# Maximum and sum of the later softmaxes by ScalarE, head by head, in the last three pairs of a chain of four transformer blocks

## The reference

```
x = x + Wo0 * attention(groupnorm(x), context)              # 8 heads of 64 (channels as tokens: 256x256 scores)
x = x + tanh(gate) * Wo1 * attention(x, layernorm(context))  # 16 heads of 16
h = rmsnorm(attention(x; keys of context and of x) + x);  x = MLP(h) + x
x = x + attention(layernorm(x))                              # self, masked
x = x + attention(layernorm(x), context)                     # cross, masked
x = x + MLP(layernorm(x))
```

## Time and profile before

| | us |
|---|---|
| median of 3 runs | 1304.58 (1303.95 to 1304.62) |
| profiled execution | 1303.31 |
| its span, first to last instruction | 1301.4 |
| mean granted clock of TensorE | 0.987 of full speed |
| TensorE busy | 1238.8 (95%) |
| VectorE busy | 1026.2 (79%) |
| ScalarE busy | 869.2 (67%) |
| GpSimd busy | 565.5 (43%) |

### The profile page before, as it was taken

The page is one execution under the profiler, slowest core; times in us unless marked ns, Lnnn a source line. Parts: engine busy times, 40 slices in busy tenths (PEclk is TensorE's granted clock), DMA queues, the critical chain, the costliest instruction groups (busy, mean ns, idle before and its releaser), DMA issues.

```text
span 1301.4 us, 35231 instructions
## 1 busy us (share of the span) xinstructions
PE 1238.8 (95%) x13116; PEld 963.6 (74%) x13116; DVE 1026.2 (79%) x2452; ACT 869.2 (67%) x2287; POOL 565.5 (43%) x977
## 2 busy tenths in 40 slices
PE   6999999999999999999999999999999999999775
PEld 4766778777777877777786777868777787868554
DVE  4778887888978787888878788787888888696753
ACT  3666677776767777776766776768676777766441
POOL 2553454264444526345344535443354453442321
PEclk9999999999999999999999999999999999999896
DMA  8100000000000000000000000000000000000000
GB/s 323 35 18 19 2 24 3 22 8 7 18 11 19 7 22 8 18 7 11 19 7 22 8 6 19 12 18 7 23 8 6 19 7 6 3 6 2 6 5 5
DMA packets 23589, 25.78 MB, mean 20 GB/s; under 512 B 10624, under 2 KB 22912, under 8 KB 23168
## 3 DMA queue, kind: packets, MB, share of 16 engines
q1 hardware_dynamic: 23424, 23.55, 5.8%
HBM read 21.44 MB, written 2.10 MB: 18 GB/s over the span
## 4 chain that ended last, share of the span: by engine, by line
PE 79%; DVE 9%; issue 5%; ACT 4%; POOL 2%; DMA 0%; SPq 0%; POOLq 0%; DVEq 0%; ACTq 0%
PE bank L687 10%; PE bank L953 8%; PE bank L513 8%; PE attended L642 8%; PE bank L627 7%; PE bank L962 7%; PE bank L693 5%; PE bank L721 5%; PE bank L502 4%; PE bank L747 4%; PE bank L710 3%; PE bank L734 3%; PE bank L680 2%; PE bank L421 2%; PE bank L738 2%
## 5 line engine op out<-in xcount | busy, mean ns | idle before, releaser
L614 POOL TENSOR_SCALAR p_a<-p_a,rec_a 128x256 f32<-128x256 f32 x512 | 244.3, 495 | 187.7 <-DVE rec_a L569 187.5
L600 ACT ACTIVATE p_a<-bank,nmax_a 128x256 f32<-128x256 f32 x512 | 236.8, 476 | 68.2 <-DVE nmax_a L563 67.5
L563 DVE TENSOR_REDUCE nmax_a<-bank 128x2 f32<-128x512 f32 x256 | 167.8, 678 | 12.6 <-PE bank L513 11.8
L627 PE MATMUL bank<-ident,p_a 128*128 128x128 f32 x1024 | 143.0, 277 | 5.6 <-POOL p_a L614 2.7
L627 PEld LDWEIGHTS bank<-ident,p_a 128*128 128x128 f32 x1024 | 114.2, 142 | 33.6 <-issue 25.2
L513 PE MATMUL bank<-k_a,q_a 64*128 64x256 f32 x1024 | 137.5, 395 | 1.2 <-ACT q_a L580 0.7
L642 PE MATMUL attended<-p_a,v_a 128*64 128x256 f32 x1024 | 133.7, 390 | 2.6 <-DVE v_a L474 1.1
L513 PEld LDWEIGHTS bank<-k_a,q_a 64*128 64x128 f32 x1024 | 92.4, 186 | 27.6 <-issue 18.8
L600 ACT ACTIVATION_READ_ACCUMULATOR p_a<-bank,nmax_a 128x1 f32 x512 | 106.0, 207 | 0.0
L642 PEld LDWEIGHTS attended<-p_a,v_a 128*64 128x64 f32 x1024 | 64.1, 136 | 55.2 <-issue 21.9
L675 ACT ACTIVATE p_a<-bank 128x512 f32<-128x512 f32 x128 | 75.8, 602 | 29.6 <-PE bank L627 28.9
(11 more groups left out here) (260 smaller groups left out, 2987.1 us busy)
## 6 DMA issues: line engine op xcount, KB each, us to landing
wb<-in_wb SPq DMA_DIRECT2D x1, 4096.0 KB, 12.3
wc<-in_wc SPq DMA_DIRECT2D x1, 4096.0 KB, 24.8
xc<-in_x SPq DMA_DIRECT2D x16, 128.0 KB, 2.7
xc<-in_ctx SPq DMA_DIRECT2D x16, 128.0 KB, 2.9
c_top<-in_ctx SPq DMA_DIRECT2D x16, 128.0 KB, 2.7
k_c<-in_ctx SPq DMA_DIRECT2D x16, 128.0 KB, 2.1
res_a<-in_x SPq DMA_DIRECT2D x16, 128.0 KB, 2.2
out<-y_out SPq DMA_DIRECT2D x16, 128.0 KB, 1.7
```

What stands on the lines that cost most here:

```text
L563: dve.tensor_reduce(nmax_a[:, n, e, :], ps[:, :].rearrange("p (q k) -> p q k", q=KT), AX.X, ALU.max, negate=True).then_inc(A.s["max"], 1)
L600: last = act.activation(p_a[:, j % 2, n, e, qt, :], ps[:, qt * D:(qt + 1) * D], ACT.Exp, bias=nmax_a[:, n, e, qt:qt + 1], accum_out=sum_a[ ...
L614: last = pool.tensor_scalar(p_a[:, j % 2, n, e, qt, :], p_a[:, j % 2, n, e, qt, :], rec_a[:, n, e, qt:qt + 1], 1.0, ALU.mult, ALU.mult)
L627: last = nc.tensor.transpose(ps[:, kt * D + qt * P:kt * D + (qt + 1) * P], p_a[:, j % 2, n, e, qt, kt * P:(kt + 1) * P], ident[:, :])
```

## The change

In the pairs from 13 on, in all four later attentions, VectorE writes the maxima negated and takes nothing off. ScalarE takes each group's exponentials in 8 instructions, one a head, each with the head's negated maximum as bias and the head's sum as accumulated output, straight into T.sum. VectorE's sum falls away; it only takes the reciprocal, waiting for the exponentials. TensorE's transposes wait for the exponentials instead of the sum. ScalarE has one further wait, for the reciprocals of the pair before. ORDER and BANK are new strings, made for this; up to pair 12 they differ from the old ones by small swaps, in the last three pairs by more.

```diff
+BY_HEAD = {"b": 13, "e": 13, "c": 13, "f": 13}
 ...
             for r in range(KT):
                 for c in range(blocks):
                     yield
-                    pe.wait_ge(T.s["sum"], T.at(i, "sum", r + 1))
+                    if by_head(T, i):
+                        pe.wait_ge(T.s["exp"], T.at(i, "exp", r + 1))
+                    else:
+                        pe.wait_ge(T.s["sum"], T.at(i, "sum", r + 1))
 ...
+        def by_head(T, i):
+            return i >= BY_HEAD[T.name]
 ...
-                dve.tensor_reduce(T.max[:, r, :], v.rearrange("p c h k -> p h c k"), AX.XY, ALU.max).then_inc(T.s["max"], 1)
+                dve.tensor_reduce(T.max[:, r, :], v.rearrange("p c h k -> p h c k"), AX.XY, ALU.max,
+                                  negate=by_head(T, i)).then_inc(T.s["max"], 1)
+                if by_head(T, i):
+                    continue
 ...
-                dve.tensor_reduce(T.sum[:, r, :], heads_of(T, r).rearrange("p c h k -> p h c k"), AX.XY, ALU.add).then_inc(T.s["sum"], 1)
-                yield
-                dve.wait_ge(T.s["sum"], T.at(i, "sum", r + 1))
+                if not by_head(T, i):
+                    dve.tensor_reduce(T.sum[:, r, :], heads_of(T, r).rearrange("p c h k -> p h c k"), AX.XY, ALU.add).then_inc(T.s["sum"], 1)
+                    yield
+                    dve.wait_ge(T.s["sum"], T.at(i, "sum", r + 1))
 ...
-                act.wait_ge(T.s["sub"], T.at(i, "sub", r + 1))
-                act.activation(T.p[:, r, :], T.p[:, r, :], ACT.Exp).then_inc(T.s["exp"], 1)
+                if by_head(T, i):
+                    act.wait_ge(T.s["max"], T.at(i, "max", r + 1))
+                    if i:
+                        act.wait_ge(T.s["rec"], T.at(i, "rec", 0))
+                    v = heads_of(T, r)
+                    for h in range(HB):
+                        last = act.activation(v[:, :, h, :], v[:, :, h, :], ACT.Exp, bias=T.max[:, r, h:h + 1], accum_out=T.sum[:, r, h:h + 1])
+                    last.then_inc(T.s["exp"], 1)
+                else:
+                    act.wait_ge(T.s["sub"], T.at(i, "sub", r + 1))
+                    act.activation(T.p[:, r, :], T.p[:, r, :], ACT.Exp).then_inc(T.s["exp"], 1)
```

More of the change, by code:

```diff
@@ L103 @@
[L103 to L112, removed]
@@ new lines @@
+        "nksnnnakaaaaaddaadddddaadkkdkdnkddsnddkkaaddksksddaaddadkdaadddnnaabddbdnadbdddaandddbbdbadkkbaedddeeeedeadddd"
+        "daddanneaebeebaaenakekdddndadbdgaggbbdggbdabcddeccceeceededdddaaaddccdaddceedaceeadefddfefnandbddbdaafdafndfdk"
+        "kkdnfagkkkkkgbgaddgghbddbcabcccbhcehdeeheecddcdecaaddadcdddhaddfannefeeeaabdebaaendddnddgdadgfddgggadffdfdaadd"
+        "fdckacckkcdckkkadbkkdddcddchaabcbdbcaabhefbdeeeedbehfnnddhheeeeaeadefddddndaddaaagdggddndffgfgkddfkckaaddddkkk"
+        "kbcddcckbhcbabanhbbchencdeeeedaecdhbcadhdeeeeaeadnfeafndddadgdfdggdaaggddffddafckkkcccfkkdbddddcdahkkbkbabhhbd"
@@ new lines @@
+        "ceaceeeehebddbdahcnnaeeceeaenddfeaddnfdgddafddggaaddggffaadfddckfkkcckkckbdacdkkddhdbdbabhhbcaeheeeedenanchddb"
+        "dacbeecdeendeadfeafnddfgddaaddggadfdfgdfdgkaakfkcddddkkkkkcbccddaahdbcdbaabhbhecceeeecenndcddhhdabeebeedaeaded"
+        "fdandfdganddfddaadggdadgfgfafdckfkkcckkkcbaahkkddddhhabbhdbcddbhbeddeeeeccdeabcnaacnddeedfdefaefddanddedaaffef"
+        "dddkfdkkndgdkkggbkggkaakddchdbabcccbdchbdeheeeeccaecabddbhhceedeaeaefnfeandfddgddggaadngfdgfddfaknkkfdddcdkkcc"
+        "cahbdhchkbkkhbhbdaccbcaaeceeeedddedaadddadffebedbeedaenneafdddagnagdddgffggnfddfckkkccckhkchhbkhkdhakdbddbcabc"
@@ new lines @@
+        "dcbdeceeeedddeddaafdfnaneeeebaebaendadnagddggfddagddgadfdafdfckkkccfckkkkkbdhcdhhdbddhbhbacbcaeceeeeceaadddddd"
+        "deefeeaefaefddnaanabddgbddaggffdgngddfankkkfcddakkcccbdkckkdhbabddhabccdhbcedheeeecheaafddfddddaefddeeeanebnfb"
+        "eddfdaaadgfaddgkakgfadkddhgdgkkdddcdabkckkhbccbhcbddahbdeheeeccedecddddcddeebfeefbfeefgfgfgkgfkkgkkkkbckhchhcc"
+        "bbcbhbhecceeeececeefeeefefgfggfggfkfccchchchhhccccfffffffhhhhh"),
+    "act": (
+        "knnakaaaasadaadaaaadaakdaakdkaadkkaaaaddaaaaadnnabadbaaadbadbabbaabdaakeadaeaddeaenneaebaeebaaaeaakaddaagbbgbb"
+        "gdaabcaeadcedcdeaacccaaaaeceeddaeeaefaanandbdfbfafafaafadkkkgaakkggbabdahbbcabachedhccecdccaaeaaddeaafnaeaeeea"
+        "nbadaebaaadgdaagdgffffaafdaadcakaakkckackcddcbchbbcbaabaaaefbaadehbhnedeneeeeaeaaddaafagafdaaggffafadkkckaaddk"
+        "kbbcbhbabacncabachehcdneacdbeeeeeeaaeaafaaaddagaggdffaadffaaafckkkckddbahbkbbcbacahechcaaebdbdaecneneeeeaeafaa"
+        "adgdaafggfaadaffadafaackkkkcabdkbdhbbcbaachcheaaenancedbdecbeeeeaaefaaadgdaafaafggffdafadkakakacdkkcdbabhbaaba"
+        "baaccecchhecnnddeebeebaeeaaeaadfadagaaddaafggfaaaffafckkkkchakabdbdahabbahbdbecdceccaabcneneaeefaeadeaadaafedf"
+        "ffaafdkaakkgdkggbbkaadhcbbaacbheccheccacbdaaebeeedeeaaefaanangdfggafadfafafakkkacddkchaabhbbhkbccbacccaeaaedde"
+        "adafaeebedaeeabaeannadgaaffdgfgfaafckkkchkhchckbbdabdabcbcaaceeddaafeneneeeebaeabaadagdaagagaadffdfafafcakkkac"
+        "kkhdbbhbdhbccbcacaecaaeaaeddeeefeeaeaaadnanabdgabffaggffaadfakkkcdakaacbbhkbbccdaahbccaceahdeaafeddeeaeeeafnfa"
+        "ebafbndfdaaagfaaagkakadgkadahkdcabbkbbachbhdcaecaecccddeefbeeeebeffgffgfgkkkkkchbbcbbhbhccecceceeeeeefefgffggf"
@@ new lines @@
+        "bbbdbabnbbabbdabaannnnabaakbbaaaddeaeeeeeeeeeeaeddeaeenadeeanenaaanaaaenannnaaeegkgkgdgdagnkknabbbbbnbbnbbgbba"
+        "gabangcccabdcabadbcaceecccceeeceeeeceeceeaadccaccdaaceeaaeacedeacafffdfaaaedafeegffffngafnffkffafnfafdndaaagng"
+        "nngnaafdnffhnaaknhnhaknhkkkkgbbbbbgbbababdbbgbcacccaacbcabbhccccchccececcceeceeddeeeeeaaecaaeacefdfdfefaaheeaa"
+        "deannfannaaaaeaaeengngngngddngaannnnaadgffffadfgfffkfgffafaccccafaadafaadfhhhchcaacccckcckacbbbcckcbbcbbcbbdbb"
+        "kdaabkckdaacbfafffbaabaaheeaeeeedeeeeeheefeeneedenhnaaneaaeeffffgggfdndnagafgknaanfaffaafafgfgaandadnnnnfagccc"
@@ new lines @@
+        "fffffffffhhhhhhh"),
+    "pool": (
+        "ssknaaaaaaaakaakaankkaaaaaaaaaaakanabbaaaeagaaeakeeaaaaaagnaabbccaaegacaeccaaccaaeeffaaaakffkffaagaanhkhaakcbc"
+        "baacaeagcceccaaffaaeeaaaagnaakffaakcffcaaaahhcaackckccbbaaffeagaeaaeeaakffkgaaaaffaanaccahhkkcbbccaageccaaefee"
+        "faaaangaakkffaaffcaacaachkhckcbbegccaaeaaeeffaagaankffkaaffaaccaaaahhckkccbbaacgceeaafeefaagaankffkaaaaffaacch"
+        "ahakkcbbccaaaaegccefeefaaaagaanakffakaaffaacchhckkaabbaaccegeccaaffeeaakffkaaffaaagahnahakkccbbcaaccegeccaaeef"
+        "faaaagkkffffacacaanhhakacaacckbbccegffaeaaaeeaaaakgkffaaffcacanhhckcckbbaccaaeagffeeeaagaanaakffkaacffcaachahk"
+        "akccbbccegaaeaaffeeaakkagffaaaffaaccnhhkaacaakccbbccaaegaaeffkffeekaaffaagaaaahhaackcaakbcbaaccegeccaaffeekffk"
+        "gffhhckckcbbccegcceffeekfgfffcchhcccccffffffhh"),
```

93 lines of the change are left out of this document (33 added, 60 removed).

## The result

The changed kernel takes **1320.89 us** (1319.9 to 1322.07), the kernel before 1304.26 us beside it on the same chip: a ratio of 1.0127, 95% interval 1.0112 to 1.0142. It is slower, as forecast, but by 16.6 us where the sum had 7.3, and so just outside the range given. The profiled execution took 1322.07 us, the slowest of its four, against 1303.31 before; so what is read from the two traces adds up to 18.7 us and not to 16.6.

What follows compares the result with a forecast made beforehand. TensorE was taken to bound the kernel, almost gapless in the middle, so the waits of the last pairs decide. Terms 0.8 + 2.1 + 0.9 + 1.1 + 3.4 - 1 = +7.3 us on the 1304.6 median gave 1312 us, range 1300 to 1320.

Steps and rivals of the forecast that it cites:

- two signs of being wrong: Stated refutations: a head takes under 0.24 us, or TensorE has no gap behind the output product of stage e, pair 14.
- E14/F13: Stage e of pair 14, f of 13: exponentials behind the last copy leave TensorE 4.1 us idle, not 0.7: +3.4 us.
- E15/C14: Stage e of pair 15 beside c of 14: 5.9 us less in the stretch, 7.0 us more ahead: +1.1 us.
- The price of a head: ScalarE's exponential for one head, start to start: 0.29 us, 2.4 a group of eight; in stage e 0.34, 2.85 a group.
- G of 15: Stage g of pair 15 beside f of 14: two table loads saved against longer exponentials and queueing: +0.9 us.
- C of 15: Stage c of pair 15, alone at the end: second group's transposes begin at 1262.4 instead of 1260.3: +2.1 us.
- F of 15: Stage f of pair 15, nothing beside it: second group's exponentials end later, delaying transposes and product: +0.8 us.
- H of 15: Last stage of pair 15, up to the span's end: no term of its own, counted as 0.
- Elsewhere: Pairs 12 to 14: work drawn forward and VectorE freed, -1 us; further up and at the start 0, within 2.
- Rival 1: Faster: short exponentials and fillers, heads of 0.23 to 0.24 us, about -3 us, 1301 us; chance 0.19.
- Rival 2: Order absorbs it: stall in stage f of pair 13 filled, start and middle give 2 back, 1304 to 1306 us; chance 0.14.
- Rival 3: Accumulator reads don't overlap with 64-column exponentials: 0.52 us a head, +18 us, 1330 us; chance 0.05.

Runs made afterwards that it cites:

- spares in both kernels: Never-read matmuls put ahead of tail steps: 73 in the changed kernel, 1307.46 us; 46 in the kernel with new order to stage e of pair 12, 1291.98 us.
- new tail: Changed kernel with old order and banks up to stage e of pair 12, new ones with exponentials by head only behind it: 1331.21 us, ratio 1.0195.
- new head: Kernel before with new order and banks up to stage e of pair 12, old ones behind, softmax unchanged: 1300.11 us against 1305.12, ratio 0.9964.

## Why the prediction was right and wrong

**Direction and places** were right: the waits moved from VectorE's sums to ScalarE's exponentials, and the gap behind e14's product is there. Neither of the two signs of being wrong came: a head is not under 0.24 us, and that gap exists. TensorE's gaps behind 1173 us grew by 9.0 us, where 7 were forecast. TensorE after, between e14's projection and g14:

```profile
1167.58 1.13 PE L751 MATMUL bank<-wb,e_yT 128*128 128x256 f32 x4 [0.93 <-DVE e_yT L801]
1171.31 1.12 PE L725 MATMUL bank<-ident,f_p 128*128 128x128 f32 x4 [2.60 <-ACT f_p L823]
...
1173.96 1.12 PE L725 MATMUL bank<-ident,f_p 128*128 128x128 f32 x4 [0.68 <-ACT f_p L823]
```

In brackets stands the idle time before: 2.60 and 0.68, and 0.16 ahead of g14's transposes between them (not shown), 3.4 us where 4.1 were forecast. The way to it was not quite the one laid out. ScalarE ended e14's copy at 1167.07 and then waited for f13's maximum, which waited for GpSimd's mask:

```profile
1166.48 2.48 POOL L857 TENSOR_TENSOR f_p<-f_p,m_add 128x512 f32<-128x512 f32 x2
1167.78 0.69 DVE L783 TENSOR_REDUCE f_max<-f_p 128x8 f32<-128x512 f32 x1 [0.25 <-POOL f_p L857]
1168.50 0.35 ACT L823 ACTIVATE f_p<-f_p,f_max 128x64 f32<-128x64 f32 x1 [1.43 <-DVE f_max L783]
```

**The step that failed is twofold: the two terms between e14 and e15 were too small, and no term had the clock.** E14/F13 and E15/C14 were laid out at +4.5 us together. They measured +13.9, and +9.9 at full clock with spares in both kernels. All terms behind e14 come to 8.3 us, where the new tail costs 15.5 at full clock. On top of that stand 5.3 us for TensorE's clock, for which the sum had nothing, since every term is counted in waits at the durations of the rows of before. The sum missed by no more than 9.3 us because the new head gives 5.0 back, where the sum had -1 for pairs 12 to 14 and nothing, within 2, for what stands ahead of them; that is luck.

What the clock does is seen behind each new gap. f13's transposes take 1.12 us for four, where eight took 1.44 in the earlier trace rows, and g14's first half 3.62. From e14's projection to e15's the stretches in the section on the result are 14.06 us apart, of which gaps are 6.5 (14.71 us of idle against 8.23) and busy time 7.6. Of those 7.6 about 0.9 is a step of f14 that fell into the stretch; the rest, 6.7, is clock (0.82 against 0.94). With spares the clock is 1.00 in both and the stretches are still 10.0 us apart, with 8.7 more of gaps and spares: part of what the slow matmuls took would have been waited for anyway.

Where the two terms were too small can be told by the mark between them, the end of b15's copy. From e14's sum to it the forecast has 3.4 us of waits and 7.0 of work moved ahead, 10.4; it is 15.1 longer (35.5 us instead of 20.4), and 12.5 with spares in both. b15's own two groups by head stand in this stretch and have no term. From the copy to e15's sum it has -5.9 (26.9 instead of 32.8); it is -1.2 (31.6), and -2.6 with spares in both (28.1 and 30.7). So the way to e15 became shorter by less than half of what was laid out.

**The price of a head** was taken as 0.29 us, it is 0.33 (e: 0.34, it is 0.39). The row it came from reads PSUM (128x256, start to start 0.45), these groups read SBUF. That this is the difference is argued, no run shows it. What the runs show is the make-up: 0.245 + 0.085. For a group it is 0.26 us more than forecast. ScalarE's total of +42 us came as worked out (43). VectorE's subtractions and sums that went away took 39.6 us added up, as worked out (40), yet its busy time fell by 26 only: its other steps took 4.4 us more, most of it small steps of the first block's group norm, and 9.1 us of the records that went lay over their neighbours, which busy time counts once.

**E of 15 beside C of 14.** ScalarE did what was laid out: gelu, both groups of c14, then e15's copy. The largest wait is in e15's own softmax:

```profile
1225.99 1.97 PE L725 MATMUL bank<-ident,e_p 128*128 128x128 f32 x8 [4.54 <-ACT e_p L823]
```

The forecast had two groups of 2.85 us in this way; they are 3.1 each, which is 0.5 of the 3.3 us that the way is longer than laid out at full clock. The rest is not traced to a step.

**G of 15**: +1.1 for +0.9, and of the three table loads one is left, as laid out. But at full clock the step costs nothing (-0.1), so that part of the agreement is luck. Counting a table load as 1.28 us and no more was right as well: in the rows by time above, the exponential starts 0.02 us behind the load's end.

**C of 15**: +4.9 for +2.1. From the second gelu to the second transposes it is 2.8, most of it the two groups at their true price (2.6); the other 2.1 is clock, and with spares the whole step is +2.8. The second transposes, the product, the transposed reciprocals and the projection took 1.11, 1.08, 0.69 and 2.08 us at the lower level, where the kernel before had 0.66, 0.65, 0.44 and 1.13.

**F of 15**: +1.6 for +0.8 (+1.7 with spares in both). The first maximum ends at 1291.38, the product starts at 1298.72:

```profile
1291.41 0.35 ACT L823 ACTIVATE f_p<-f_p,f_max 128x64 f32<-128x64 f32 x1 [6.84 <-DVE f_max L783]
...
1296.87 1.12 PE L725 MATMUL bank<-ident,f_p 128*128 128x128 f32 x4 [1.54 <-ACT f_p L823]
...
1298.72 1.08 PE L738 MATMUL bank<-f_p,f_v 128*32 128x64 f32 x32 [0.73 <-issue]
```

7.3 us where 5.7 were before and 6.5 forecast; twice 0.26 is most of what is missing. **H of 15**, +1.3 where nothing was said, is clock alone: the same 32 matmuls of its first half took 6.50 us instead of 5.18, and with spares in both kernels nothing is left.

**Elsewhere**: -4.2 by e14 where -1 was taken, and -5.0 by the new head alone. The start is part of it: in the first 100 us TensorE is busy 87.9 instead of 86.0, in the next 96.8 instead of 96.1. For it the prediction had "0, within +-2". Which of the small swaps win the rest stays open.

**The rivals.** Rival 1 should decide from a group of 1.9 us. The kernel without reads has groups of 1.95, and is still 10 us slower than before. That speaks against its turning point, but it is no clean test, since it keeps VectorE's sums behind the groups. Rival 2 had its mechanism, the order giving back, and it is real: 20 of 37 us; only not enough. Rival 3 fell: reads and exponentials overlap.

What stays open: how much of the 9.9 us between e14 and e15 at full clock is the groups' length and how much the order of the tail. The kernel with the old softmax in the new order loses 10.5 us there, at its own low clock, but its joined steps spoil the test. At c15 and f15, 4.5 us at full clock, it is the groups.

## What to carry to other kernels

Where stages wait for one another, price a new gap twice: the wait itself and the work behind it at the lower clock, which here was 5 us on top of 15; matmuls that nobody reads, as many as fit into the gaps and no more, gave 8 to 13 us back. An instruction that replaces two others is no gain if it is longer on an engine whose fixed queue other stages share: six groups of b, 2 us longer each, cost 15.9 us, the largest waits among them for copies and exponentials of other stages behind them. And test an order and an edit made for each other apart, and the order in parts: the new head with the old tail beats both kernels.

## What the runs showed of the hardware

- The granted clock fell to 0.50, 1.2 GHz, where TensorE was busy 9.9 of 23 us in short pieces, and stood at 0.99 to 1.00 over the last 100 us when spare matmuls filled most gaps. The fill must fit: 84 spares in the kernel before gave 2.1 us, while 46 in the one with the new head gave 8.1; 133 in the kernel after gave 6.3, 73 gave 13.4.
- A read of the accumulator takes 0.19 us, starts 0.1 us before the exponential's end, and sets the next start back by 0.085 us.
- A matmul of 256 columns in float32, two instructions, took 0.43 us at the full clock.
